# Context stage of the mixer: the keys' low word by a subtraction on GpSimd instead of a product with the negated identity

## The reference

```python
q = split_heads(query @ Wq.T + bq)
k = split_heads(key @ Wk.T + bk)
v = split_heads(value @ Wv.T + bv)
scores = jnp.einsum('bhqd,bhkd->bhqk', q, k) / np.sqrt(HEAD_DIM)
```

```python
dA = jnp.exp(jnp.einsum('bld,dn->lbdn', delta, A))
dBu = jnp.einsum('bld,bln,bdl->lbdn', delta, B, u)
carry = a * carry + bu          # over l
y = jnp.einsum('bdn,bn->bd', carry, c)
```

## Time and profile before

| | |
|---|---|
| median of 3 runs | 1975.14 us (1968.61 to 1975.64) |
| span of the profiled execution | 1970.9 us; the page gives no other time of it |
| PE (TensorE) busy | 1777.7 us, 90% |
| DVE (VectorE) busy | 1452.0 us, 74% |
| ACT (ScalarE) busy | 1175.0 us, 60% |
| POOL (GpSimd) busy | 366.9 us, 19% |
| first and last unit's scan starts | 383.51 us, 697.30 us |

### The profile page before, as it was taken

One profiled execution on the slowest core, in us unless ns is written; L12 is line 12 of the kernel. 1 busy time (PEld: TensorE's weight loads), 2 busy tenths in 40 slices (PEclk: granted clock), 3 DMA queues, 4 the chain that ended last, 5 costly groups with the idle time before them and its releaser, 6 DMA issues. The chain is left out here.

```text
span 1970.9 us, 32747 instructions
## 1 busy us (share of the span) xinstructions
PE 1777.7 (90%) x12553; PEld 1220.2 (62%) x12553; DVE 1452.0 (74%) x1685; ACT 1175.0 (60%) x2100; POOL 366.9 (19%) x238
## 2 busy tenths in 40 slices
PE   7988998999989957999988899999999999998754
PEld 5877776467757745878776455555555555546424
DVE  7637552587898855565656699999999999974474
ACT  1332333577687734343431588889888898873363
POOL 4223201054545402222212000010010000000000
PEclk8999998999999988999989799999999999998877
DMA  9798862158948831121227556575566655400000
GB/s 360 278 329 314 312 223 81 45 199 289 321 172 314 315 117 44 67 76 62 70 36 137 136 107 129 93 135 112 108 117 116 115 112 98 102 21 6 0 0 22
DMA packets 171768, 280.19 MB, mean 142 GB/s; under 512 B 21422, under 2 KB 100430, under 8 KB 164446
## 3 DMA queue, kind: packets, MB, share of 16 engines
q1 hardware_dynamic: 169886, 277.61, 49.6%
q10 hardware_dynamic: 1728, 0.49, 0.1%
HBM read 187.46 MB, written 88.14 MB: 140 GB/s over the span
## 5 line engine op out<-in xcount | busy, mean ns | idle before, releaser
L2300 DVE TENSOR_REDUCE xn_peaks<-psum 128x2 f32<-128x1024 f32 x512 | 621.2, 1224 | 43.7 <-PE psum L2107 35.8
L2257 ACT ACTIVATE moe_mix_transposed<-psum 128x512 f32<-128x512 f32 x1024 | 552.8, 597 | 73.2 <-PE psum L2112 27.1
L2112 PE MATMUL psum<-xn_q_stack,xn_k_words 50*128 50x256 f32 x2048 | 378.9, 307 | 12.7 <-ACT xn_q_whole L2231 7.3
L2112 PEld LDWEIGHTS psum<-xn_q_stack,xn_k_words 50*128 50x128 f32 x2048 | 251.1, 187 | 215.8 <-ACT moe_mix_transposed L2257 187.3
L2107 PE MATMUL psum<-xn_k_words,xn_q_stack 50*128 50x512 f32 x1024 | 374.0, 452 | 5.2 <-DMA xn_q_stack<-q_rows 3.1
L2144 PE MATMUL psum<-moe_mix_transposed,xn_v 128*32 128x256 f32 x4096 | 329.9, 394 | 1.9 <-issue 0.3
L2107 PEld LDWEIGHTS psum<-xn_k_words,xn_q_stack 50*128 50x128 f32 x1024 | 186.4, 186 | 12.9 <-DVE xn_peaks L2300 7.8
L931 POOL TENSOR_TENSOR mx_state<-mx_du,mx_b_all_channels 128x1024 f32<-128x1024 f32 x64 | 154.1, 2408 | 197.8 <-ACT mx_b_all_channels L1108 85.1
L1189 DVE TENSOR_TENSOR_SCAN mx_state<-psum,mx_state 128x1024 f32<-128x1024 f32 x64 | 146.2, 2284 | 49.3 <-ACT psum L1118 41.7
L322 PE MATMUL psum<-xw_ctx_natural,xw_weights_transposed 128*128 128x256 f32 x512 | 124.4, 388 | 13.4 <-DVE xw_weights_transposed L474 13.2
L2144 PEld LDWEIGHTS psum<-moe_mix_transposed,xn_v 128*32 128x32 f32 x4096 | 81.9, 108 | 73.9 <-issue 8.8
(11 more groups left out here) (331 smaller groups left out, 2579.6 us busy)
## 6 DMA issues: line engine op xcount, KB each, us to landing
xn_k_words<-k_words SPq DMA_DIRECT2D x384, 128.0 KB, 6.4
ctx_words<-xw_ctx_transposed_words SPq DMA_DIRECT2D x64, 512.0 KB, 7.1
ctx_chunk_words<-ctx_words SPq DMA_DIRECT2D x64, 512.0 KB, 5.5
k_words<-ctx_k_words SPq DMA_DIRECT2D x128, 256.0 KB, 2.5
v_all<-ctx_v SPq DMA_DIRECT2D x32, 544.0 KB, 3.4
xn_v<-v_all SPq DMA_DIRECT2D x32, 544.0 KB, 5.0
xw_mask<-in_mask_BxSxS_ik SPq DMA_DIRECT2D x8, 2048.0 KB, 7.7
xw_ctx_natural<-in_ctx SPq DMA_DIRECT2D x32, 512.0 KB, 6.6
```

What stands on the lines that cost most here:

```text
L2112: return pe.matmul(PS[:, narrow_bank("exp", n, step, a), half * S:(half + 1) * S], K[n % XN_KSLOTS][narrow_rows(a), kt * P:(kt + 1) * P], ...
L2257: act.activation(t["weights"][:, step % 4, a, :, :], bank.rearrange("p (t s) -> p t s", t=2), ACT.Exp, scale=XN_SCALE).then_inc(s.taken, 1)
L2300: dve.tensor_reduce(t["peaks"][:, m % 2, q, :, c], PS[:, 2 * (x % 2):2 * (x % 2) + 2, :], AX.X, ALU.max).then_inc(s.top_read, 1)
```

## The change

The product with the negated identity goes, and with it the identity's negative and the list of chunks whose remainder stood alone. ScalarE writes both of its results right behind each other: the high word, and the full value with bias into a new tile `ctx_k_whole`. GpSimd subtracts the one from the other (`low`) and the store waits for that (`kl0`, `kl1`). GpSimd does `low` behind the inputs of the next unit.

```diff
-CTX_ALONE = 0, 1, 2, 17, 18
...
-         "minus": sb("minus_identity", [P, P], F32R), "chunk": sb("raw_weights", [P, KD, BANK]),
+         "whole": sb("k_whole", [P, 2, BANK]), "chunk": sb("raw_weights", [P, KD, BANK]),
...
     def store_keys(i, m):
-        sp.wait_ge(kr[m], 2 * i + 2)
+        sp.wait_ge((s.kl0, s.kl1)[m], i + 1)
...
-    pool.tensor_scalar(t["minus"][:], k.ident[:], -1.0, None, ALU.mult).then_inc(s.words, 1)
...
+    def low(i, m):
+        pool.wait_ge(sems[2][m], 2 * i + 2)
+        pool.tensor_tensor(t["keys"][:, m, 1, :], t["whole"][:, m, :], t["keys"][:, m, 0, :].bitcast(F32), ALU.subtract
+                           ).then_inc((s.kl0, s.kl1)[m], 1)
+
+    def step(n):
+        if n % 4 in (1, 2):
+            low(n // 4, n % 4 - 1)
+
+    return Steps(step)
...
-    def remainder(i, m):
-        pe.wait_ge(kr[m], 2 * i + 1)
-        pe.matmul(PS[:, bank("keys", i, m), :], t["minus"][:], t["keys"][:, m, 0, :], start=False, stop=True,
-                  skip_group_check=True).then_inc(kp[m], 1)
...
     def rounded(i, m, n):
-        act.wait_ge(kp[m], 2 * i + n + 1)
+        act.wait_ge(kp[m], i + 1)
         if n == 0 and i:
             act.wait_ge(ks[m], 32 * i)
-        act.activation(t["keys"][:, m, n, :], k.PS[:, bank("keys", i, m), :], ACT.Identity,
+        act.activation(t["whole"][:, m, :] if n else t["keys"][:, m, 0, :], k.PS[:, bank("keys", i, m), :], ACT.Identity,
                        bias=t["bk"][:, m:m + 1]).then_inc(kr[m], 1)
...
     for i in range(MX_UNITS):
         inputs(i)
+        if i:
+            ctx.upto(mx_context(i - 1, 1))
+    ctx.upto(CTX_STEPS)
```

More of the change, by code:

```diff
@@ L605, in context_sems @@
 def context_sems(k):
-    s = k.sems("ctx", "weights words in0 in1 vp vc vs kp0 kp1 kr0 kr1 ks0 ks1 v_ones")
+    s = k.sems("ctx", "weights words in0 in1 vp vc vs kp0 kp1 kr0 kr1 kl0 kl1 ks0 ks1 v_ones")
     return s, (s.kp0, s.kp1), (s.kr0, s.kr1), (s.ks0, s.ks1)
@@ L669, in context_pool @@
         pool.tensor_copy(w2[:, 0, :, :], w).then_inc(s.words, 1)
-        pool.wait_ge(s.words, 2 * n + 2)
+        pool.wait_ge(s.words, 2 * n + 1)
         pool.tensor_tensor(w2[:, 1, :, :], w, w2[:, 0, :, :].bitcast(F32), ALU.subtract).then_inc(s.words, 1)
+    def low(i, m):
[6 more added lines that the diff above has]
+    return Steps(step)
 def context_pe(k, t, sems, bank, free):
@@ L679, in keys @@
         if i == 0:
-            pe.wait_ge(s.words, 5)
+            pe.wait_ge(s.words, 4)
         free("keys", i, m)
@@ L701, in step @@
         i, sub = n // 4, n % 4
-        if i in CTX_ALONE and sub < 2:
+        if sub < 2:
             keys(i, sub)
[L704 to L711, removed]
         elif sub == 2:
             values(i, 0)
-            remainder(i, 1)
         else:
@@ L744, in step @@
         i, sub = n // 4, n % 4
-        if i in CTX_ALONE and sub < 2:
+        if sub < 2:
             rounded(i, sub, 0)
             rounded(i, sub, 1)
[L748 to L754, removed]
         elif sub == 2:
             values(i, 0)
-            rounded(i, 1, 1)
         else:
@@ L916, in mixer_pool @@
     pool.memset(t["xpad"][:, :, :, 0:MX_PAD], 0.0).then_inc(s.clear, 1)
-    context_pool(k, ct, cs)
+    ctx = context_pool(k, ct, cs)
     def inputs(i):
```

## The result

The changed kernel takes **2027.36 us** (median of 4 runs, 2026.0 to 2033.89) against 1972.56 us for the kernel before (4 runs, 1968.61 to 1975.64): a ratio of 1.0288, 95% interval 1.0265 to 1.0311, or +54.8 us. It is slower. The forecast was 2034 us, 1995 to 2060.

What follows compares the result with a forecast made beforehand. VectorE's port exclusion with GpSimd, plus late key stores, was taken to bound the changed kernel: A 4 + B 25.4 + C 1 + D 29.3 = +59.7 us on 1970.9, plus 4.2, forecast 2034 us, range 1995 to 2060.

Steps and rivals of the forecast that it cites:

- B and D: Mixer stretches of units 8 to 31 (121.5 us) and 40 to 62 (105.1 us); forecast to grow 25.4 and 29.3 us.
- the port: GpSimd's subtractions and VectorE's products exclude one another; forecast +14.9 us in units 8 to 31, +24.8 from unit 40.
- the chain: Keys' store waits for the subtraction, ScalarE's next rounding for that store; forecast +10.5 and +4.5 us in B and D.
- Removal counts for nothing once TensorE isn't last: Dropping TensorE's 64 products, priced at 12.4 us plus 9, gains only while TensorE and ScalarE set the pace.
- 1.22 us of exclusion for each subtraction: In B and D, two subtractions lengthen a pair of units from 7.95 to 10.4 us; lower end 1.08 each.
- the walk: Step-by-step timing of a pair of units on VectorE and GpSimd: 7.95 us now, 10.4 us with two subtractions.
- The store's wait costs 1.5 us in ten places: Where rounding and late store fall in neighbouring units, seven in B, three in D: 1.5 us each, between 0 and 3.0.
- A +4, C +1: Units 0 to 7 grow 4 us (late store, subtractions, less products saved); units 32 to 39 grow 1 us.
- Rival 1: In the mixer the port bounds but the store loop does not: +42 us, 2017 us; chance 0.28.
- Rival 2: Subtraction does not shut VectorE out or finds it waiting, TensorE keeps the pace: -12 to -18, 1960 us; chance 0.08.
- Rival 3: Both at half size in B and D: +20 less up to 15 from TensorE, +5, 1980 us; chance 0.05.
- Rival 4: More waits: loads queued behind late stores, or TensorE's clock falling in pauses: +37 more, 2070 us; chance 0.12.

Runs made afterwards that it cites:

- run 3: The kernel before, products kept, plus 64 GpSimd subtractions on spare data at the change's places, nothing waiting for them: 1.0099 of the kernel before.
- run 8: The changed kernel without its subtraction (low word left out), plus 64 spare GpSimd subtractions that nobody waits for: 1.0104 of the kernel before.
- run 4: The changed kernel without the subtraction, low word left out, so only TensorE's 64 products are removed: 0.9909 of the kernel before.
- run 5: The changed kernel with GpSimd's subtractions one unit earlier, same operations, buffer and queue: 1.0106 of the kernel before.
- run 2: The changed kernel with each subtraction replaced by three GpSimd memsets of about the same length, order, waits and stores kept: 1.0196 of the kernel before.
- run 9: The changed kernel with V stores and chunk loads issued by ScalarE, leaving SyncE the keys' stores alone: 1.0486 of the kernel before.
- run 10: The changed kernel with V stores and chunk loads issued by ScalarE and two sets of key buffers: 1.0120 of the kernel before.
- run 6: The changed kernel with SyncE issuing the load of chunk i+2 ahead of chunk i's second keys store: 1.0363 of the kernel before.

## Why the prediction was right, and where its steps were not

Direction and total were right, +54.8 us against +59.7, but two large terms were wrong in opposite directions: in B and D the port was put at 39.7 us and costs 18.8 over the kernel before, the chain was put at 15.0 and costs 33.0 on top. That the total came out within 5 us is luck.

- **Removal counts for nothing once TensorE isn't last.** Right as stated: runs 3 and 8, with and without the products, have the same B and D. The 12.4 us that I priced it at in B and D, and the 9 in A and C, were too much: run 4 gained 8.3 and 7.2 there.
- **1.22 us of exclusion for each subtraction.** Too large, and even the "lower end" of 1.08 was: 0.83 against the walk's own base, 0.94 by VectorE's busy time. B + D with unit 63 came to 270.3 us in the working, 266.3 without it; run 8 has 245.4. Against the kernel before that is +18.8 us in the two stretches, where the terms said 14.9 + 24.8. The walk had charged a blocked operation its full length after the holder's end and had nothing of a subtraction under a scan; the trace has 1.1 us of it there (651.81) and 1.1 us instead of 1.27 left after the release. These two bring a pair to 9.86. What is between its 0.95 and 0.83 wasn't followed.
- **The store's wait costs 1.5 us in ten places, "the other steps ... nothing more".** This failed most. The mechanism was right: the roundings' wait, in the first place named (unit 10 to 11, 7.76 us apart), with stores landing in 2.4 us in the median (2.5 forecast). In the ten places the scans are 8.5 us apart in the mean, not 10.65; but five others (units 41, 45, 49, 50, 59) have 7.3 to 8.0 us as well. The chain costs 17.8 us in B (145.2 - 127.4) and 15.2 in D (133.2 - 118.0), where I had 10.5 and 4.5. Units u and u+1 of the seven places in B together are 12.3 us longer than in run 8, those of the three in D 7.6: 2.0 us in the mean where I had 1.5. The rest, 5.5 us in B and half of D's loss, lies in steps that I had priced at nothing.
- **A +4, C +1.** Measured +3.6 and +0.8. In A run 4 shows the saving (4.4; I had 5.4), run 8 the exclusion (+2.1 over it), and the change 5.9 more for the late store.
- **Rival 1, the port only.** Its time, 2017, was wrong with the 1.22: run 8 puts it at 1.0104 x 1972.56 = 1993. **Rival 2** would have needed a free subtraction; its -12 to -18 us is run 4, with -15.6 in the stretches. **Rival 3** is the nearest to what the port alone does (+20 in B and D at half size: +18.8 measured). **Rival 4** was half there: loads late behind the stores, 45.4 us of TensorE's waits. The other half, the clock, shows as 0.94 in B and 0.92 in D for 1.00 before, with TensorE waiting; in run 5 it is 0.96 and 0.97, in run 4 1.00. TensorE is busy 229.5 us in B and D for products that took it 213.2 in run 4, 16.3 us more, so the lower clock may be a part of what the chain costs. How much of it reaches the time wasn't isolated; runs 8 and 5 differ in it (1.00 and 0.96 in B) by 1.6 us there.
- **The skill's resume time.** By the Trainium skill (SBUF — State Buffer, A bandwidth-pool intuition that's wrong) some 7 us came on top. The page measured that figure on descriptors that GpSimd writes. Run 8's rows don't show it: L1187 ends 1.09 us after its blocker, less than its 1.20 alone.
- **The signs named ahead.** SyncE's stores of keys wait 287.7 us for GpSimd and none for ScalarE: as said. TensorE fell to 83% and 82% in B and D. "VectorE two units in 10.4 us" was wrong (11.6 in D in the mean; 10.3 in run 8), and VectorE's busy share fell (B 82% to 72%) instead of rising, which is what tells the chain from the port: in run 8 it rose to 98%.

## What to carry to other kernels

When work moves to an idle engine, ask first who waits for its result, and how late in that engine's order it stands: here one unit of delay cost more than all contention, and one line (run 5) gave it back. A wait in front of a store blocks everything behind it in an in-order queue, so freeing one link only hands the stall to the next; a total that comes out right says nothing of its terms until the terms are run apart.

## What the runs showed of the hardware

- VectorE operations with two SBUF operands and GpSimd operations that read SBUF take the port in turns, and one that was shut out finishes in a little less than its time alone: L1187 in 1.09 us after the release (1.20 alone), a 128x512 subtraction in 1.1 (1.27 alone). The profile counts the shut-out time as busy: in run 8 L673's mean is 1938 ns, L1187's 1888, L1192's 1496, against 1266, 1462 and 682.
- GpSimd's memsets did not lengthen VectorE's operations (run 2: L1190 1458 ns, L1195 682; run 4, without them, 1462 and 682).
- Issuing two loads of 512 KB held ScalarE's queue for 1.4 to 2.3 us in run 9 (up to 3.1 in run 10), and a V store of 544 KB for 0.34 to 0.38.
- A 45.4 us wait of TensorE for loads could be removed entirely and the kernel still got slower (run 6): TensorE waited 45.2 us for ScalarE instead. A wait that goes away is a gain only if no other takes its place.
